# A 30-step recurrent stage: the wide mix, the ten-step Newton chain, and products and transposes in blocks

## The chip, the cores and the metric

The kernel runs on one core of one Trainium2 chip, in one launch. The metric is the device time of that core in microseconds (us), median of a few runs. The core has five engines that each work through their own instructions in order and wait for each other by semaphores: TensorE (PE in the profile, its weight loads are PEld), VectorE (DVE), ScalarE (ACT), GpSimd (POOL) and SyncE (SP), which here only issues DMAs. A DMA is a transfer by one of 16 DMA engines.

## The reference

A graph transformer of two layers on 128 graphs of 128 nodes with 128 channels, all fp32: attention and a mixture of experts in the first layer, attention and a recurrent feed-forward in the second. Only the last part is touched by the change:

```python
def step(h, _):
    h = h + 0.01 * jnp.tanh(h)
    h = h * jax.nn.sigmoid(h)
    h = _layernorm(h, ln_w, ln_b)      # (h - mean) * rsqrt(var + 1e-5) * w + bias, over the channels
    h = jnp.einsum('bsc,dc->bsd', h, W) + b
    return (h, None)
x, _ = jax.lax.scan(step, x, None, length=30)      # then added to the input of this part
```

Each of the 128 x 128 tokens goes through 30 steps, independently of all others.

## The kernel before

The stage is `recurrent_ffn`. The state of all tokens stays in SBUF as `g`, channels on partitions, in 16 chunks of 1024 tokens. A **slot** is one chunk in one of the 30 steps: slot s is step s // 16, chunk c = s % 16, 480 slots in all. An iteration is 16 slots; iterations 0, 1 and the closing one (number 30) are unrolled, 2 to 29 are a loop on every engine. A chunk has two units u = 0, 1 of 512 tokens, one PSUM bank each.

The layernorm is folded: its mean and weight go into the matrix `w_main` beforehand, and only the reciprocal standard deviation of each token (rstd) remains to be applied. What a slot s does:

- **product** (PE, L1253, one fp32 matmul of 128 x 512 per unit, two rows in the trace): `p_y` = `w_main` times the scaled state. `p_y` has room for two slots, so it waits for the mix of slot s - 2 (`bank_taken`), and for POOL's scaling.
- **tanh** (ACT, L1308, per unit): `th` = tanh(`p_y` + bias).
- **mix** (DVE, L1132, per unit, 512 wide): `th` = 0.01 `th` + `p_y`.
- **silu** (ACT, L1312, per unit): writes the new state `g`.
- **transposes** (PE, L1267, four of 128 x 128 per unit): tokens onto partitions, into `p_gt`, which has room for one slot. So the transposes of slot s, unit u, wait for the statistics of slot s - 1, unit u, and for the silu.
- **statistics** (DVE, L1139, two instructions of 256 per unit): the variance parts of 512 tokens.

Four chunks are a **group** of 32 token columns. When its statistics are there, DVE works out rstd by an integer first guess and three Newton steps, a chain of 11 small instructions n = 0 to 10 on 128 x 32 (`newton`, L1147 to L1161), each waiting for the one before. Then PE transposes rstd (L1273, `transpose_rstd`), ACT copies it (L1335), SP stores it to DRAM and reads it back spread over all partitions (`rb`), and POOL multiplies the four chunks of `g` by it (L1074). All that has to be done before the products of the next step, 16 slots later.

The order on each engine is written out by hand. In turn c, working on slot s, before the change: PE does product(s,0), transposes(s-2,0), product(s,1), transposes(s-2,1), and when c % 4 == 1 the transpose of rstd. DVE does mix(s-1,1), statistics(s-2,0), two Newton instructions, mix(s,0), statistics(s-2,1), two Newton instructions. ACT does tanh(s,0), silu(s-1,1), tanh(s,1), silu(s,0). Newton instructions of a group stand in the turns with c % 4 = 2, 3 and 0: four, four and three.

Of the kernel before, what the change touches and what calls it, by code (L numbers as in the profile page):

```python
# [935 lines left out]
def recurrent_ffn(nc, env, x_sb, out_dram, ln_w, ln_b, w_dram, b_dram, N_TILES=128, ITERS=30):  # L936
# [11 lines left out]
    CHAIN, XCHAIN = 11, 12  # L948
    MAGIC = 1597463007.0
    OUTS = 4  # L950

    with ExitStack() as ctx:
# [20 lines left out]
        rstd = sb("rstd", [P, GTILES])  # L973
        rstd_row = sb("rstd_row", [GTILES, 2, P])
# [62 lines left out]
        with nc.Block() as block:  # L1037
# [52 lines left out]
            def _(dve):  # L1090
# [52 lines left out]
                def newton(k, q, n):  # L1143

                    if n == 0:
# [3 lines left out]
                    else:  # L1149
                        dve.wait_ge(s_nw, CHAIN * k + n)  # L1150
                        if n == 1:
                            wait(dve, s_rt, k)
                            ins = nc.vector.tensor_scalar(rstd[:].bitcast(I32), v.bitcast(I32), -0.5, MAGIC,
                                                          ALU.mult, ALU.add)
                        elif n % 3 == 2:
                            ins = nc.vector.tensor_tensor(work, v, rstd[:], ALU.mult)  # L1156
                        elif n % 3 == 0:
                            ins = nc.vector.scalar_tensor_tensor(out=work, in0=work, scalar=-0.5, in1=rstd[:],  # L1158
                                                                 op0=ALU.mult, op1=ALU.mult)
                        else:  # L1160
                            ins = nc.vector.scalar_tensor_tensor(out=rstd[:], in0=work, scalar=1.5, in1=rstd[:],  # L1161
                                                                 op0=ALU.add, op1=ALU.mult)
                    ins.then_inc(s_nw, 1)

                def newton_part(i, c, place):

                    k, q = GROUPS * i + (c - 6) // GC, (c - 6) // GC % GROUPS
                    for n in range(4 * ((c - 6) % GC) + 2 * place, 4 * ((c - 6) % GC) + 2 * place + 2):
                        if n < CHAIN and live_group(k):
                            newton(k, q, n)  # L1170

# [243 lines left out]
```

## Time and profile before

| | us |
|---|---|
| median of 3 runs | 3339.24 (3337.21 to 3339.80) |
| the profiled execution, its own time | 3341.66 |
| its span, first to last instruction | 3339.9 |
| recurrent stage, from about 1800 us to the end | about 1540 |

The busy shares over the whole span (PE 93%, DVE 87%, ACT 71%, POOL 52%) mix the four parts of the model; the change is in the last part alone, so its own stretch is what has to be read. A row of the timeline gives start and duration of an instruction (or of several alike), and in brackets how long its engine sat idle before it and what released it. On DVE and ACT the next instruction starts before the last one's duration is over, so what an instruction costs its engine is the distance of two starts, while who waits for it waits for its end.

### The profile page before, as it was taken

How to read it: one execution, taken by the hardware profiler on the slowest of the kernel's cores; microseconds unless marked ns; L12 is line 12 of the kernel's file. 1: busy time of each engine (PE TensorE's matmuls, PEld its weight loads, DVE VectorE, ACT ScalarE, POOL GpSimd, SP SyncE). 2: the span in 40 equal slices, each digit the busy share in tenths (PEclk: the TensorE clock that was granted, in tenths of full speed). 3: DMA queues.
4: the chain of work that ended last, by engine and by line, in shares of the span. 5: the costliest groups of instructions: out<-in, count | busy, mean ns of one | idle time of the engine just before them, and what ended most of it. 6: DMA issues, size and time to landing. Idle time of an engine off the chain costs nothing. (4 is left out here: it accounts for less than half of the span.)

```text
span 3339.9 us, 67477 instructions
## 1 busy us (share of the span) xinstructions
PE 3091.6 (93%) x16801; PEld 2062.9 (62%) x16801; DVE 2915.5 (87%) x8976; ACT 2377.9 (71%) x4988; POOL 1722.7 (52%) x1101
## 2 busy tenths in 40 slices
PE   7989986999998999999995799999999999999998
PEld 4666665888886777777774544444444444444446
DVE  5777776888887888888887799999999999999997
ACT  4666663444444777777776988888888888888883
POOL 2445444333332111121110388888888877777776
PEclk9999998999999999999996799999999999999999
DMA  4000000000000000000000255454555555454447
GB/s 129 16 16 16 19 13 14 1 0 0 0 0 17 14 13 9 13 13 13 9 6 3 81 182 176 174 174 176 177 177 177 177 177 177 177 177 176 172 173 239
DMA packets 135072, 290.04 MB, mean 87 GB/s; under 512 B 12081, under 2 KB 69601, under 8 KB 135009
## 3 DMA queue, kind: packets, MB, share of 16 engines
q1 hardware_dynamic: 118112, 280.89, 24.5%
q10 hardware_dynamic: 16896, 8.39, 0.9%
q8 instruction: 29, 0.48, 0.1%
q14 instruction: 35, 0.28, 0.0%
HBM read 278.88 MB, written 10.35 MB: 87 GB/s over the span
## 5 line engine op out<-in xcount | busy, mean ns | idle before, releaser
L1074 POOL TENSOR_TENSOR d_g<-d_g,d_rb 128x1024 f32<-128x1024 f32 x480 | 1120.6, 2369 | 380.6 <-DMA d_rb<-d_rstd_rows 380.2
L1253 PE MATMUL d_p_y<-d_g,d_w_main 128*128 128x512 f32 x1856 | 953.2, 595 | 0.1
L1267 PEld LDWEIGHTS d_p_gt<-ident,d_g 128*128 128x128 f32 x3840 | 436.6, 142 | 710.2 <-ACT d_g L1312 657.1
L1312 ACT ACTIVATE d_g<-d_th,d_bias 128x512 f32<-128x512 f32 x928 | 669.7, 722 | 182.1 <-DVE d_th L1132 174.7
L1139 DVE BATCH_NORM_STATS2 d_stats<-d_p_gt 128x6 f32<-128x256 f32 x1920 | 725.1, 419 | 23.1 <-PE d_p_gt L1267 23.0
L1132 DVE SCALAR_TENSOR_TENSOR d_th<-d_th,d_p_y 128x512 f32<-128x512 f32 x960 | 652.3, 680 | 14.2 <-ACT d_th L1308 7.9
L1267 PE MATMUL d_p_gt<-ident,d_g 128*128 128x128 f32 x3840 | 602.3, 280 | 64.9 <-ACT d_g L1312 23.1
L1308 ACT ACTIVATE d_th<-d_p_y,d_bias 128x512 f32<-128x512 f32 x928 | 622.0, 670 | 1.1 <-PE d_p_y L1253 1.0
L514 ACT ACTIVATE a_prob<-a_masked,a_neg_max 128x128 f32<-128x128 f32 x1024 | 327.4, 392 | 111.8 <-DVE a_neg_max L334 111.7
L434 PE MATMUL a_p_s<-a_k_heads,a_q_t 128*128 128x512 f32 x768 | 397.0, 599 | 0.6 <-DVE a_k_heads L310 0.6
L451 PEld LDWEIGHTS a_p_pv<-a_v_ones,a_prob_t 128*128 128x128 f32 x3072 | 375.1, 193 | 10.7 <-issue 10.3
L451 PE MATMUL a_p_pv<-a_v_ones,a_prob_t 128*128 128x17 f32 (+1 forms) x3072 | 376.7, 259 | 3.2 <-DVE a_context L347 2.0
L817 DVE SCALAR_TENSOR_TENSOR x_sb<-m_p_y,m_combine,x_sb 128x128 f32 (+1 forms) x1024 | 311.4, 343 | 68.1 <-PE m_p_y L859 55.2
L906 ACT ACTIVATE m_hidden<-m_p_h,m_cols 128x512 f32<-128x512 f32 x256 | 176.5, 689 | 225.9 <-PE m_p_h L851 225.9
L441 PEld LDWEIGHTS a_p_pt<-ident,a_prob 128*128 128x128 f32 x1536 | 192.4, 141 | 201.6 <-issue 198.5
L1253 PEld LDWEIGHTS d_p_y<-d_g,d_w_main 128*128 128x128 f32 x1856 | 280.4, 191 | 7.2 <-issue 5.7
L859 PEld LDWEIGHTS m_p_y<-m_w_sb,m_hidden 128*128 128x128 f32 x2048 | 266.0, 191 | 25.8 <-issue 3.5
L859 PE MATMUL m_p_y<-m_w_sb,m_hidden 128*128 128x128 f32 x2048 | 270.9, 275 | 0.0
L321 DVE TENSOR_TENSOR a_masked<-a_p_s,a_mask 128x512 f32<-128x512 f32 x256 | 176.1, 688 | 83.7 <-PE a_p_s L434 82.6
L248 POOL TENSOR_TENSOR x_sb<-x_sb,a_out_bias 128x512 f32 (+1 forms) x32 | 42.1, 1316 | 385.7 <-DVE a_masked L321 339.3
L527 ACT COPY a_prob_t<-a_p_pt 128x512 f32<-128x512 f32 x384 | 221.7, 577 | 17.0 <-PE a_p_pt L441 17.0
L230 POOL TENSOR_TENSOR a_rstd<-a_var,minus_half 128x4 f32<-128x4 f32 x64 | 66.3, 1037 | 323.0 <-DVE a_var L292 323.0
(167 smaller groups left out, 4443.7 us busy)
## 6 DMA issues: line engine op xcount, KB each, us to landing
d_rb<-d_rstd_rows SPq DMA_DIRECT2D x480, 512.0 KB, 5.5
a_adj_in<-in_adj_dram SPq DMA_DIRECT2D x64, 256.0 KB, 2.8
out_dram<-d_out_sb ACTq DMA_DIRECT2D x32, 256.0 KB, 3.2
d_rstd_rows<-d_rstd_row SPq DMA_DIRECT2D x120, 16.0 KB, 1.4
m_w_sb<-in_L_ffn_w_dram SPq DMA_DIRECT2D x2, 512.0 KB
x_sb<-in_x_dram SPq DMA_DIRECT2D x1, 256.0 KB, 2.9
a_w_raw<-in_L_gnn_Wq_dram SPq DMA_DIRECT2D x2, 64.0 KB, 2.2
a_w_raw<-in_L_gnn_Wk_dram SPq DMA_DIRECT2D x2, 64.0 KB, 2.1
```

Of the source, the lines that this page charges most:

```text
L434: nc.tensor.matmul(p_s[:, u % 2], q_t[:, par, g * P:(g + 1) * P], k_heads[:, par, g, h0:h0 + HU, :], start=mask_on_vector, stop=True).then ...
L451: last = nc.tensor.matmul(p_pv[:, h, :], prob_t[:, u % 2, h, :], v_ones[:, par, g, h0 + h, :], start=True, stop=True)
L514: last = nc.scalar.activation(prob[:, u % 2, h, :], scores_src[:, u % 2, h, :], ACT.Exp, bias=neg_max[:, u % 2, h:h + 1], scale=EXP_SCALE)
L817: last = nc.vector.scalar_tensor_tensor(out=x_tile, in0=p_y[:, e % 2, t, :], scalar=combine[:, par, t, e:e + 1], in1=x_tile, op0=ALU.mult, ...
L859: last = nc.tensor.matmul(p_y[:, e % 2, t, :], hidden[:, e % 2, t * P:(t + 1) * P], w2_sb[:, e, :], start=True, stop=True)
L1074: nc.gpsimd.tensor_tensor(g[:, c, :], g[:, c, :], rb[:, buf, :], ALU.mult).then_inc(s_gs, 1)
L1132: nc.vector.scalar_tensor_tensor(out=th[:, b, cols(u)], in0=th[:, b, cols(u)], scalar=0.01, in1=p_y[:, b, cols(u)], op0=ALU.mult, op1=ALU. ...
L1139: ins = nc.vector.bn_stats(stats[:, q % 2, (j * CT + t) // 2].rearrange("p a s -> p (a s)"), p_gt[:, t * P:(t + 2) * P].rearrange("p (a c) ...
L1253: nc.tensor.matmul(p_y[:, c % 2, cols(u)], w_main[:], g[:, c, cols(u)], start=True, stop=True).then_inc(s_y, 1)
L1267: ins = nc.tensor.transpose(p_gt[:, t * P:(t + 1) * P], g[:, c, t * P:(t + 1) * P], ident[:])
L1308: nc.scalar.activation(th[:, b, cols(u)], p_y[:, b, cols(u)], ACT.Tanh, bias=col).then_inc(s_th, 1)
L1312: nc.scalar.activation(g[:, c, cols(u)], th[:, c % 2, cols(u)], ACT.Silu, bias=col).then_inc(s_g, 1)
```

## The change

- **Mix 1024 wide.** One instruction for both units. The products of slot s + 2 and both silus of slot s now wait for that one mix, and the mix for the second tanh.
- **A chain of ten.** The first Newton steps are replaced by one step of higher order and a last one of the old kind; a factor of 3/8 is moved into `w_main`. Ten instructions with one PSUM operand on the reading side at most, one at a time in three places of a turn instead of two and two, so that other work stands between any two of them. They take the turns with c % 4 = 2, 3, 0 (three each), and the last, n = 9, stands in the turn with c % 4 = 1, behind statistics(s-2,0).
- **Blocks.** PE: product(s,0), product(s,1), transposes(s-2,0), transposes(s-2,1), transpose of rstd. DVE: statistics(s-2,0), Newton, mix(s), Newton, statistics(s-2,1), Newton. ACT: the copy of rstd, tanh(s,0), tanh(s,1), silu(s-1,0), silu(s-1,1).
- In the closing iteration both halves of a result are added one behind the other.

```diff
-    CHAIN, XCHAIN = 11, 12
+    CHAIN, XCHAIN, PLACES = 10, 12, 3
...
-                def mix(s, b, u):
-                    dve.wait_ge(s_th, units(s, u))
-                    nc.vector.scalar_tensor_tensor(out=th[:, b, cols(u)], in0=th[:, b, cols(u)], scalar=0.01,
-                                                   in1=p_y[:, b, cols(u)], op0=ALU.mult, op1=ALU.add).then_inc(s_u, 1)
+                def mix(s, b):
+                    dve.wait_ge(s_th, units(s, UNITS - 1))
+                    nc.vector.scalar_tensor_tensor(out=th[:, b], in0=th[:, b], scalar=0.01, in1=p_y[:, b],
+                                                   op0=ALU.mult, op1=ALU.add).then_inc(s_u, 1)
...
-                    for n in range(4 * ((c - 6) % GC) + 2 * place, 4 * ((c - 6) % GC) + 2 * place + 2):
-                        if n < CHAIN and live_group(k):
-                            newton(k, q, n)
+                    n = PLACES * ((c - 6) % GC) + place
+                    if n < CHAIN and live_group(k):
+                        newton(k, q, n)
...
                         s = CHUNKS * i + c
-                        if live(s - 1):
-                            mix(s - 1, (c - 1) % 2, 1)
-                        elif last(i):
-                            add_x(c - 1, 1)
                         if live(s - 2):
                             statistics(s - 2, (c - 2) % CHUNKS, 0)
                         newton_part(i, c, 0)
                         if live(s):
-                            mix(s, c % 2, 0)
+                            mix(s, c % 2)
                         else:
                             add_x(c, 0)
+                            add_x(c, 1)
+                        newton_part(i, c, 1)
                         if live(s - 2):
                             statistics(s - 2, (c - 2) % CHUNKS, 1)
-                        newton_part(i, c, 1)
+                        newton_part(i, c, 2)
...
-                        wait(pe, s_u, units(s - 2, u))
+                        wait(pe, s_u, s - 1)
...
-                            if live(s - 2):
+                        if live(s - 2):
+                            for u in range(UNITS):
                                 transpose_g(s - 2, (c - 2) % CHUNKS, u)
...
-                        if live(s):
-                            tanh(s, c % 2, 1, col)
-                            silu(s, c, 0, col)
+                        for u in range(UNITS):
+                            if live(s):
+                                tanh(s, c % 2, u, col)
+                        for u in range(UNITS):
+                            if live(s - 1):
+                                silu(s - 1, (c - 1) % CHUNKS, u, 0.0 if isinstance(i, int) and s - 1 < CHUNKS else bias[:])
```

DVE's row in the loop, in a turn with Newton instructions (c = 3). Names are those of the program: `d_stats` the statistics, `d_p_nw` and `d_rstd` the Newton chain, `d_th` the mix; register instructions set the values that waits compare with. Before:

```order
L1139 BN_STATS d_stats<-d_p_gt 128x6 [waits d_g_transposed]
L1139 BN_STATS d_stats<-d_p_gt 128x6
L1150 REGISTER_ALU
L1161 SCALAR_TENSOR_TENSOR d_rstd<-d_p_nw,d_rstd 128x32 [waits d_newton_chain]
L1150 REGISTER_ALU
L1156 TENSOR_TENSOR d_p_nw<-d_p_nw,d_rstd 128x32 [waits d_newton_chain]
L1131 ISA
L1132 SCALAR_TENSOR_TENSOR d_th<-d_th,d_p_y 128x512 [waits d_tanh_ready]
L1139 BN_STATS d_stats<-d_p_gt 128x6 [waits d_g_transposed]
L1139 BN_STATS d_stats<-d_p_gt 128x6
```

The same turn after (`d_vy` is the new tile `vy2`):

```order
L1142 BN_STATS d_stats<-d_p_gt 128x6 [waits d_g_transposed]
L1142 BN_STATS d_stats<-d_p_gt 128x6
L1155 REGISTER_ALU
L1162 TENSOR_TENSOR d_vy<-d_p_nw,d_rstd 128x32 [waits d_newton_chain]
L1134 ISA
L1135 SCALAR_TENSOR_TENSOR d_th<-d_th,d_p_y 128x1024 [waits d_tanh_ready]
L1155 REGISTER_ALU
L1164 SCALAR_TENSOR_TENSOR d_p_nw<-d_vy,d_p_nw 128x32 [waits d_newton_chain]
L1142 BN_STATS d_stats<-d_p_gt 128x6 [waits d_g_transposed]
L1142 BN_STATS d_stats<-d_p_gt 128x6
```

The pair of linked Newton instructions has become one on each side of a mix that is twice as wide.

PE's row in the loop around the transpose of rstd (`d_p_row`), from the second half of turn c = 1. Before:

```order
L1253 MATMUL d_p_y<-d_g,d_w_main 128x512 [waits d_g_scaled,d_u_ready]
L1267 MATMUL d_p_gt<-ident,d_g 128x128 [waits d_stats_ready,d_g_ready]
L1267 MATMUL d_p_gt<-ident,d_g 128x128 x3
L1271 ISA
L1018 REGISTER_ALU [waits d_newton_chain]
L1273 MATMUL d_p_row<-ident,d_rstd 32x128 [waits d_row_ready]
L1018 ISA
L1252 REGISTER_ALU [waits d_u_ready]
L1253 MATMUL d_p_y<-d_g,d_w_main 128x512 [waits d_g_scaled]
L1267 MATMUL d_p_gt<-ident,d_g 128x128 [waits d_stats_ready,d_g_ready]
L1267 MATMUL d_p_gt<-ident,d_g 128x128 x3
```

After:

```order
L1275 MATMUL d_p_gt<-ident,d_g 128x128 [waits d_stats_ready,d_g_ready]
L1275 MATMUL d_p_gt<-ident,d_g 128x128 x3
L1272 REGISTER_ALU
L1275 MATMUL d_p_gt<-ident,d_g 128x128 [waits d_stats_ready,d_g_ready]
L1275 MATMUL d_p_gt<-ident,d_g 128x128 x3
L1279 ISA
L1021 REGISTER_ALU [waits d_newton_chain]
L1281 MATMUL d_p_row<-ident,d_rstd 32x128 [waits d_row_ready]
L1021 REGISTER_ALU
L1260 REGISTER_ALU [waits d_u_ready]
L1261 MATMUL d_p_y<-d_g,d_w_main 128x512 [waits d_g_scaled]
L1261 MATMUL d_p_y<-d_g,d_w_main 128x512 [waits d_g_scaled,d_u_ready]
```

Behind the transpose of rstd there now stand both products of the next slot, and only then its transposes.

## Rows read from the trace of the kernel before

**Rows 1.** Windows: length, busy (count) of each engine, TensorE's granted clock, DMA.

```profile
1850.00:1900.00 50.00, 32.42 (x153) 26.35 (x154) 32.38 (x99) 45.48 (x104) 16.20 (x7) 0.68 0.24 86
...
2500.00:2600.00 100.00, 95.46 (x412) 48.77 (x411) 97.88 (x292) 87.37 (x144) 83.58 (x37) 1.00 0.49 172
```

**Rows 2.** Groups by line, 1900 to 3300: count | busy, mean ns | idle before.

```profile
L1074 POOL TENSOR_TENSOR d_g<-d_g,d_rb 128x1024 f32<-128x1024 f32 x466 | 1088.1, 2370 | 277.6 <-DMA d_rb<-d_rstd_rows 277.2
...
L1312 ACT ACTIVATE d_g<-d_th,d_bias 128x512 f32<-128x512 f32 x927 | 669.0, 722 | 181.9 <-DVE d_th L1132 174.6
```

**Rows 3.** Timeline of DVE, a turn with two linked Newton instructions.

```profile
2602.15 0.76 DVE L1139 BATCH_NORM_STATS2 d_stats<-d_p_gt 128x6 f32<-128x256 f32 x2
2602.82 0.17 DVE L1161 SCALAR_TENSOR_TENSOR d_rstd<-d_p_nw,d_rstd 128x32 f32<-128x32 f32 x1
2603.03 0.20 DVE L1156 TENSOR_TENSOR d_p_nw<-d_p_nw,d_rstd 128x32 f32<-128x32 f32 x1
2603.15 0.69 DVE L1132 SCALAR_TENSOR_TENSOR d_th<-d_th,d_p_y 128x512 f32<-128x512 f32 x1
2603.75 0.76 DVE L1139 BATCH_NORM_STATS2 d_stats<-d_p_gt 128x6 f32<-128x256 f32 x2
```

**Rows 4.** Timeline of DVE, a Newton instruction that stands alone.

```profile
2620.05 0.18 DVE L1161 SCALAR_TENSOR_TENSOR d_rstd<-d_p_nw,d_rstd 128x32 f32<-128x32 f32 x1
2620.14 0.68 DVE L1132 SCALAR_TENSOR_TENSOR d_th<-d_th,d_p_y 128x512 f32<-128x512 f32 x1
```

**Rows 5.** Timeline of DVE: the same first Newton instruction, one iteration apart.

```profile
2599.61 0.19 DVE L1147 TENSOR_SCALAR d_p_nw<-d_stats 128x32 f32<-128x32 f32 x1
...
2647.72 0.18 DVE L1147 TENSOR_SCALAR d_p_nw<-d_stats 128x32 f32<-128x32 f32 x1
```

**Rows 6.** Timeline of DVE at the loop's branch, between two iterations.

```profile
2616.64 0.19 DVE L1161 SCALAR_TENSOR_TENSOR d_rstd<-d_p_nw,d_rstd 128x32 f32<-128x32 f32 x1
...
2617.16 0.69 DVE L1132 SCALAR_TENSOR_TENSOR d_th<-d_th,d_p_y 128x512 f32<-128x512 f32 x1 [0.32 <-issue]
```

**Rows 7.** Timeline of PE, products and transposes back to back.

```profile
2608.54 1.02 PE L1253 MATMUL d_p_y<-d_g,d_w_main 128*128 128x512 f32 x2
2609.40 0.60 PE L1267 MATMUL d_p_gt<-ident,d_g 128*128 128x128 f32 x4
2609.84 1.02 PE L1253 MATMUL d_p_y<-d_g,d_w_main 128*128 128x512 f32 x2
```

**Rows 8.** Timeline, weight load of transposes that waited; transposes behind it.

```profile
2603.02 0.42 PEld L1267 LDWEIGHTS d_p_gt<-ident,d_g 128*128 128x128 f32 x4 [0.90 <-ACT d_g L1312]
...
2603.05 0.63 PE L1267 MATMUL d_p_gt<-ident,d_g 128*128 128x128 f32 x4
```

**Rows 9.** Timeline, transposes released by statistics, and the product behind them.

```profile
2616.10 0.41 DVE L1139 BATCH_NORM_STATS2 d_stats<-d_p_gt 128x6 f32<-128x256 f32 x1
...
2616.56 0.42 PEld L1267 LDWEIGHTS d_p_gt<-ident,d_g 128*128 128x128 f32 x4 [0.91 <-DVE d_stats L1139]
...
2617.06 0.59 PE L1253 MATMUL d_p_y<-d_g,d_w_main 128*128 128x512 f32 x1
```

**Rows 10.** Closing iteration, DVE and PE: the transpose of rstd waits for Newton.

```profile
3307.07 0.18 DVE L1161 SCALAR_TENSOR_TENSOR d_rstd<-d_p_nw,d_rstd 128x32 f32<-128x32 f32 x1
...
3307.30 0.10 PEld L1273 LDWEIGHTS d_p_row<-ident,d_rstd 128*32 128x32 f32 x1 [3.91 <-DVE d_rstd L1161]
...
3307.49 0.47 PE L1259 MATMUL d_p_y<-d_w_main,d_g 128*128 128x128 f32 x1
```

**Rows 11.** Timeline of PE, transposes and then the product across the loop's branch.

```profile
2613.46 0.63 PE L1267 MATMUL d_p_gt<-ident,d_g 128*128 128x128 f32 x4
2614.06 0.69 PE L1253 MATMUL d_p_y<-d_g,d_w_main 128*128 128x512 f32 x1
```

**Rows 12.** Timeline of ACT in iteration 0.

```profile
1870.92 0.60 ACT L1308 ACTIVATE d_th<-d_p_y 128x512 f32<-128x512 f32 x1 [0.43 <-PE d_p_y L1248]
...
1871.77 0.63 ACT L1312 ACTIVATE d_g<-d_th 128x512 f32<-128x512 f32 x1 [0.26 <-DVE d_th L1132]
```

More of the change, by code:

```diff
@@ L947, in recurrent_ffn @@
     ALL_GROUPS = ITERS * GROUPS
-    CHAIN, XCHAIN = 11, 12
+    CHAIN, XCHAIN, PLACES = 10, 12, 3
     MAGIC = 1597463007.0
+    RSTD_SCALE = 3.0 / 8.0
     OUTS = 4
@@ L973, in recurrent_ffn @@
         rstd = sb("rstd", [P, GTILES])
+        vy2 = sb("vy2", [P, GTILES])
         rstd_row = sb("rstd_row", [GTILES, 2, P])
@@ L1143, in newton @@
                 def newton(k, q, n):
+                    y = rstd[:]
                     if n == 0:
@@ L1152, in newton @@
                             wait(dve, s_rt, k)
[L1153 to L1158, printed above, removed]
+                            ins = nc.vector.tensor_scalar(y.bitcast(I32), v.bitcast(I32), -0.5, MAGIC, ALU.mult, ALU.add)
+                        elif n == 2 or n == 7:
+                            ins = nc.vector.tensor_tensor(work, v, y, ALU.mult)
+                        elif n == 3:
+                            ins = nc.vector.tensor_tensor(vy2[:], work, y, ALU.mult)
+                        elif n == 4:
+                            ins = nc.vector.scalar_tensor_tensor(out=work, in0=vy2[:], scalar=-10.0 / 3.0, in1=work,
+                                                                 op0=ALU.add, op1=ALU.mult)
+                        elif n == 5:
+                            ins = nc.vector.tensor_tensor(work, work, y, ALU.mult)
+                        elif n == 8:
+                            ins = nc.vector.scalar_tensor_tensor(out=work, in0=work, scalar=-0.5 * RSTD_SCALE ** 2, in1=y,
                                                                  op0=ALU.mult, op1=ALU.mult)
                         else:
-                            ins = nc.vector.scalar_tensor_tensor(out=rstd[:], in0=work, scalar=1.5, in1=rstd[:],
+                            ins = nc.vector.scalar_tensor_tensor(out=y, in0=work, scalar=5.0 if n == 6 else 1.5, in1=y,
                                                                  op0=ALU.add, op1=ALU.mult)
@@ L1174, in add_x @@
                     dve.wait_ge(s_y, units(SLOTS + o, u))
+                    dve.wait_ge(s_xb, CHUNKS)
                     wait(dve, s_out[n % OUTS], 16 * (n // OUTS))
@@ L1215, in _ @@
                 link(nc.vector.tensor_scalar(row_sum[:], row_sum[:], 1.0 / P, None, ALU.mult))
-                link(nc.vector.tensor_scalar(w_centred[:], w_centred[:], row_sum[:], float(np.sqrt(P)),
+                link(nc.vector.tensor_scalar(w_centred[:], w_centred[:], row_sum[:], RSTD_SCALE * float(np.sqrt(P)),
                                              ALU.subtract, ALU.mult))
@@ L1226, in _ @@
                 iterations(dve, body)
-                dve.wait_ge(s_xb, CHUNKS)
-                add_x(CHUNKS - 1, 1)
             @block.tensor
@@ L1310, in silu @@
                 def silu(s, c, u, col):
-                    act.wait_ge(s_u, units(s, u))
+                    act.wait_ge(s_u, s + 1)
                     nc.scalar.activation(g[:, c, cols(u)], th[:, c % 2, cols(u)], ACT.Silu, bias=col).then_inc(s_g, 1)
@@ L1324, in body @@
                         s = CHUNKS * i + c
-                        if live(s):
-                            tanh(s, c % 2, 0, col)
-                        if live(s - 1):
-                            silu(s - 1, (c - 1) % CHUNKS, 1, 0.0 if isinstance(i, int) and s - 1 < CHUNKS else bias[:])
                         k, q = GROUPS * i + (c - 10) // GC, (c - 10) // GC % GROUPS
```

1 line of the change is left out of this document (removed).

## The prediction, made before the changed kernel was run

> **What bounds the kernel now.** I read the windows first: they say which part of the kernel a stretch is like. From 1900 us on DVE is busy 97.88 us of 100, PE 95.46, ACT 87.37, at TensorE's full clock, 1.00 or 2.4 GHz [rows 1]. The groups of the same stretch say who waits: ACT's silu sat idle 181.9 us, nearly all of it for the mix on DVE, while POOL's 277.6 us of idle time were waits for its own DMAs [rows 2]. So DVE is asked, and POOL is ahead. The timeline of DVE says what a turn costs it, by distances of starts: a statistics pair 0.67 (2602.15 to 2602.82), the first of two linked Newton instructions 0.21, the second 0.12, a mix 0.60 [rows 3]; a Newton instruction alone 0.09 [rows 4]. There is no gap: 1.60 us per unit with two Newton instructions. A group of four slots is 8 x 0.60 + 8 x 0.67 + 5 pairs x 0.33 + 0.09 = 11.9. An iteration of four groups takes 2647.72 - 2599.61 = 48.11 us [rows 5]; 4 x 11.9 is 47.6, and the loop's branch adds 0.52 - 0.12 = 0.4 [rows 6]. PE has less: a product unit 0.86 and a transposes unit 0.44 [rows 7], 8 x 1.30 + 0.11 for the transpose of rstd = 10.5 per group. DVE is the bound, and PE stands 1.4 behind it.
>
> **The change part by part, on DVE.** Mix: a mix of 512 costs 0.60 and a statistics instruction of 256 half of 0.67, so 256 elements more cost 0.265, and 512 more 0.53: 1.13 per slot in place of 1.20. Its bounds are 1.10 and 1.20 (nothing saved). Newton: ten single instructions with other work between them, at 0.09 to 0.12 each; 0.10 to 0.11 in what follows. The chain's 5 x 0.33 + 0.09 = 1.74 becomes 1.05. A group is then 8 x 0.67 + 4 x 1.13 + 1.05 = 10.9, one us less. The branch, which now follows a single Newton instruction whose wait is met early, should be hidden under the statistics before it: another 0.4 per iteration. If DVE stayed the bound, an iteration would be 43.7 us. That is what must be tested against the waits.
>
> On VectorE I weigh a rule. The starts show that a linked Newton instruction costs 0.21 and an unlinked one 0.09 to 0.12, although each lasts 0.17 to 0.20 [rows 3, 4]. The Trainium skill says otherwise ("VectorE: DVE Perf Modes", on the DRAIN after every op): the next operation does not start before the pipe is empty, and waiting by semaphore costs nothing extra, so only the number of instructions counts. By it every Newton instruction would cost its whole 0.18: DVE's group would be 11.7 instead of 10.9, and the five Newton instructions on the loop below would make it 0.4 longer, which is 29 x 2.0 = 58 us, 3397. The trace does not agree with it at either place, so it gets no chance of its own, and the sum goes by the rows.
>
> **On PE and between the engines.** Group k is slots 4k to 4k + 3. Four rules of the new order matter. Transposes(s,1) wait for statistics(s-1,1), as before, since `p_gt` holds one slot. Behind transposes(s-1,1) on PE there now stand both products of slot s + 2, and only then transposes(s,0). DVE in turn s + 2 starts with statistics(s,0), so it cannot go on without them. And the transpose of rstd stands behind transposes(4k+7,1), waits for n = 9, and has the products of slot 4k + 10 behind it; before, the last Newton instruction was done two units earlier, and nobody waited.
>
> This makes a loop. I add it up, from the start of n = 9 of one group to that of the next.
>
> Leg A, n = 9 to statistics(4k+8,0). The Newton instruction lasts 0.18. From its end to the weight load of the transpose of rstd it is 0.05 in the one place of the trace where PE waited for it (3307.25 to 3307.30 [rows 10]); in the loop the wait stands in a register instruction ahead of it, and the nearest row for a two-stage release is the weight load at 2603.02, 0.11 after the statistics that ended at 2602.91 [rows 3, 8]. I take 0.11. From there to the product 0.19 [rows 10], with two register instructions between them now that the closing iteration does not have: 0.19 to 0.30, taken as 0.23, near the measured end. Two units of product 2 x 0.86 = 1.72, transposes 0.60 [rows 7], to DVE 0.05 (2603.05 + 0.63 to 2603.75 bounds it at 0.07 [rows 8, 3]). Sum 2.89. In that time DVE has 0.09 + 1.13 + 0.67 = 1.9 us of work: it waits 1.0 us.
>
> Leg B, DVE: statistics 0.67, n = 0 0.10, mix 1.13, n = 1 0.11, statistics(4k+8,1) to its end 0.76. Sum 2.77.
>
> Leg C, that end to statistics(4k+10,0): release 0.11 (0.05 where only one semaphore is waited for: 2616.51 to 2616.56), weight load to product 0.50 (2616.56 to 2617.06 [rows 9]), products 1.72, transposes and release 0.65. Sum 2.98. DVE has 2.8 us of work there: it waits 0.15 to 0.2.
>
> Leg D, DVE: 0.67, n = 6 0.10, mix 1.13, n = 7 0.11, 0.67, n = 8 0.10, 0.67, and n = 9 starts. Sum 3.45.
>
> A to D are 12.09 us per group, against 11.9 on DVE before. Four groups are 48.36; PE's own branch lies on leg C once per iteration and costs 0.60 - 0.46 = 0.14 [rows 11]. So 48.50 per iteration against 48.11: **+0.39**, times 29 iterations of this kind = +11.3 us. DVE's saving of 4.4 us per iteration is turned into its waiting.
>
> **Covered or unchanged.** ACT: four units of 0.63 each and the copy, 10.3 per group, each tanh pair ready well before its mix. The wide mix makes silu(s,0) wait for both halves, but silu(s,0) now comes a turn later, with over 1 us to spare. POOL needs rstd 16 slots later, and its idle time stays. Iteration 0 is bound by ACT, whose waits of 0.43 and 0.26 per slot [rows 12] change their places, since the second half's transposes are now not behind the first half's statistics work, but no silu fills the gap; I take 0, with -5 to +5 us for 16 slots. The closing iteration is bound by stores and by the way of the last rstd; 0, with +-2.
>
> **The sum.** The profiled execution took 3341.66 in all, 2.4 above the median of the runs. 3341.7 + 11.3 = 3353.0, and against the median 3339.2 + 11.3 = 3350.5. I predict 3350.
>
> **Rivals.**
>
> *The loop closes faster (not slower).* If the register wait costs no more than the plain one (0.05), the product follows at 0.19, and the release in leg C is 0.05, legs A and C lose 0.16 per group: 11.93, 47.86 per iteration, -7 us. A mix at 1.10 and Newton instructions at 0.09 lose another 0.1 to 0.15: 11.8, 47.3, -23. For it: 0.05 has been seen in both places. Against it: those were waits of one plain semaphore, and the unlike places are exactly those in the loop. Typical: 3332.
>
> *DVE stays the bound (faster).* If statistics(s,0) finds its transposes done, because PE is far enough ahead, the iteration is 43.7 to 44.2: 29 x -4.2 = -120, 3220 us. For it: PE has 10.5 of work per 10.9. Against it: PE cannot be ahead; it is held by statistics(s-1,1) and by n = 9, both of which DVE issues just before.
>
> *Waits cost more (slower by 1%).* Each leg has two hand-overs, and after one the first instructions may start late: at the loop's branch the mix came 0.4 late, although nothing but its issue held it [rows 6], because that could only begin behind the linked Newton instruction. Of such a delay 0.12 in leg A and 0.12 in leg C are 0.25 per group, 49.5 per iteration, +40: 3380. It decides if the product starts later than 0.45 after n = 9 ended. A lower TensorE clock would do the same; in iteration 0, with PE busy 32.42 of 50 us, it was granted 0.68 [rows 1], a mix of 1.2 and 2.4 GHz. Here PE keeps 10.5 of 12.1 us, as before, so that is a small part of it.
>
> *The change does not do on DVE what it says:* the wide mix costs 1.20, no gain. It lies on legs B and D: +0.14 per group, +16 us more, 3366.
>
> **How the numbers follow.** Around 0.2% (6.7 us) is what a measurement of this kernel can tell from no change. Chances: the loop as added up 0.57 (3338 to 3362, of which 0.45 is slower and 0.12 the same); it closes faster 0.22 (0.12 the same, 0.10 faster); DVE stays the bound 0.05; waits cost more 0.11; the wide mix saves nothing 0.05. So faster 0.15, same 0.24, slower 0.61. The range takes in both bounds of the loop, 3326 to 3368; outside are DVE as the bound and most of the costly waits, about 0.15.
>
> **What would show it.** In the timeline of DVE in the loop: a statistics pair with 0.8 to 1.1 us of idle time before it, released by PE's transposes, once per group, behind n = 9, and one of 0.1 to 0.3 two slots later; Newton instructions alone at 0.09 to 0.12; mixes 1.13 before the next start; first Newton instructions 12.1 apart. PE's weight load for rstd waits 0.3 to 0.4 us for n = 9. DVE's busy share falls from 98 to about 90 of 100. Wrong if DVE shows no idle time, if PE's wait for n = 9 is missing, or if an iteration is not 48.1 to 48.9.

## The result, and the profile after

| | before, us | changed, us |
|---|---|---|
| median of 7 runs | 3339.24 | 3351.14 (3348.86 to 3352.08) |
| ratio | | 1.0034, 95% interval 1.0022 to 1.0045 |
| span of the profiled execution | 3339.9 | 3347.1 |
| one iteration of the loop | 48.11 | 48.40 |

The changed kernel is slower by 0.34%; 3350 was predicted. An iteration here and below is the distance of the same first Newton instruction, averaged over 25 iterations of the profiled execution.

The window of [rows 1] and the groups that answer to [rows 2]: length, busy us (count) of PE, PE's weight loads, DVE, ACT, POOL, then clock and DMA; for groups count | busy, mean ns | idle before, and releaser.

```profile
2500.00:2600.00 100.00, 94.21 (x409) 53.20 (x406) 91.10 (x250) 86.16 (x141) 82.76 (x37) 1.00 0.50 176
```

```profile
L1142 DVE BATCH_NORM_STATS2 d_stats<-d_p_gt 128x6 f32<-128x256 f32 x1852 | 698.1, 418 | 126.5 <-PE d_p_gt L1275 115.8
L1317 ACT ACTIVATE d_th<-d_p_y,d_bias 128x512 f32<-128x512 f32 x924 | 633.1, 685 | 196.2 <-PE d_p_y L1261 180.5
L1321 ACT ACTIVATE d_g<-d_th,d_bias 128x512 f32<-128x512 f32 x927 | 613.1, 711 | 0.7 <-DVE d_th L1135 0.7
```

DVE fell from 97.88 to 91.10 us of 100, and no engine rose, PE's weight loads apart (48.77 to 53.20 us): nobody is the bound now. The silu, idle 181.9 us before [rows 2], now 0.7, waits no more; instead the statistics wait for PE's transposes and the tanh for PE's products. The first Newton instructions that answer to [rows 5] (timeline of DVE; an iteration from the first to the last, and the group that holds the loop's branch in the middle):

```profile
2592.24 0.19 DVE L1152 TENSOR_SCALAR d_p_nw<-d_stats 128x32 f32<-128x32 f32 x1
...
2616.26 0.19 DVE L1152 TENSOR_SCALAR d_p_nw<-d_stats 128x32 f32<-128x32 f32 x1
...
2628.62 0.19 DVE L1152 TENSOR_SCALAR d_p_nw<-d_stats 128x32 f32<-128x32 f32 x1
2640.63 0.19 DVE L1152 TENSOR_SCALAR d_p_nw<-d_stats 128x32 f32<-128x32 f32 x1
```

The timeline of DVE and PE (start, duration, engine, line, operation, in brackets the idle time before and its releaser) shows one group:

```profile
2600.72 0.17 DVE L1172 SCALAR_TENSOR_TENSOR d_rstd<-d_p_nw,d_rstd 128x32 f32<-128x32 f32 x1
2600.81 1.21 DVE L1135 SCALAR_TENSOR_TENSOR d_th<-d_th,d_p_y 128x1024 f32<-128x1024 f32 x1
2601.93 0.75 DVE L1142 BATCH_NORM_STATS2 d_stats<-d_p_gt 128x6 f32<-128x256 f32 x2
2603.57 0.76 DVE L1142 BATCH_NORM_STATS2 d_stats<-d_p_gt 128x6 f32<-128x256 f32 x2 [0.89 <-PE d_p_gt L1275]
2604.25 0.18 DVE L1152 TENSOR_SCALAR d_p_nw<-d_stats 128x32 f32<-128x32 f32 x1
2604.35 1.21 DVE L1135 SCALAR_TENSOR_TENSOR d_th<-d_th,d_p_y 128x1024 f32<-128x1024 f32 x1
2605.58 0.75 DVE L1142 BATCH_NORM_STATS2 d_stats<-d_p_gt 128x6 f32<-128x256 f32 x2
...
2609.00 0.18 DVE L1167 TENSOR_TENSOR d_p_nw<-d_p_nw,d_rstd 128x32 f32<-128x32 f32 x1
2609.29 0.76 DVE L1142 BATCH_NORM_STATS2 d_stats<-d_p_gt 128x6 f32<-128x256 f32 x2
```

```profile
2600.94 0.09 PEld L1281 LDWEIGHTS d_p_row<-ident,d_rstd 128*32 128x32 f32 x1 [0.37 <-DVE d_rstd L1172]
```

```profile
2600.94 0.28 PE L1281 MATMUL d_p_row<-ident,d_rstd 128*32 128x128 f32 x1
2601.12 1.98 PE L1261 MATMUL d_p_y<-d_g,d_w_main 128*128 128x512 f32 x4
2602.93 1.04 PE L1275 MATMUL d_p_gt<-ident,d_g 128*128 128x128 f32 x8
...
2606.47 0.63 PE L1275 MATMUL d_p_gt<-ident,d_g 128*128 128x128 f32 x4 [0.34 <-DVE d_stats L1142]
2606.94 1.88 PE L1261 MATMUL d_p_y<-d_g,d_w_main 128*128 128x512 f32 x4
2608.66 1.20 PE L1275 MATMUL d_p_gt<-ident,d_g 128*128 128x128 f32 x8
```

The last Newton instruction (2600.72) releases the transpose of rstd (2600.94), two products and the transposes follow, and only then can DVE start the statistics at 2603.57, after 0.89 idle. From the statistics that end at 2605.58 + 0.75 = 2606.33 the same way is gone again, to 2609.29, where DVE loses another 0.2 (2609.00 to 2609.29 is 0.29, of which the Newton instruction is 0.09).

### The profile page after: what moved, and what is told of

It is laid out like the page before. It is cut to its first block and busy times, and to the rows that moved or that the text cites. A ratio compares the mean times of both kernels' runs of the same rounds, so it can differ in the third digit from the quotient of the medians.

```text
span 3347.1 us, 67133 instructions
## 1 busy us (share of the span) xinstructions
PE 3077.4 (92%) x16801; PEld 2125.3 (63%) x16801; DVE 2822.2 (84%) x8376; ACT 2368.7 (71%) x4988; POOL 1720.5 (51%) x1101
## 5 line engine op out<-in xcount | busy, mean ns | idle before, releaser
L1261 PE MATMUL d_p_y<-d_g,d_w_main 128*128 128x512 f32 x1856 | 887.8, 601 | 0.1
L1317 ACT ACTIVATE d_th<-d_p_y,d_bias 128x512 f32<-128x512 f32 x928 | 635.9, 685 | 199.0 <-PE d_p_y L1261 183.3
L1275 PEld LDWEIGHTS d_p_gt<-ident,d_g 128*128 128x128 f32 x3840 | 453.1, 143 | 375.7 <-issue 326.5
L1275 PE MATMUL d_p_gt<-ident,d_g 128*128 128x128 f32 x3840 | 566.5, 279 | 66.6 <-DVE d_stats L1142 66.6
L1321 ACT ACTIVATE d_g<-d_th,d_bias 128x512 f32<-128x512 f32 x928 | 613.7, 711 | 0.7 <-DVE d_th L1135 0.7
L1135 DVE SCALAR_TENSOR_TENSOR d_th<-d_th,d_p_y 128x1024 f32<-128x1024 f32 x480 | 580.1, 1209 | 3.8 <-ACT d_th L1317 3.8
L1261 PEld LDWEIGHTS d_p_y<-d_g,d_w_main 128*128 128x128 f32 x1856 | 316.3, 190 | 238.5 <-issue 230.2
L441 PE MATMUL a_p_pt<-ident,a_prob 128*128 128x128 f32 x1536 | 230.5, 273 | 0.3 <-ACT a_prob_t L527 0.3
```

Of the source, the lines that this page charges most:

```text
L441: last = nc.tensor.transpose(p_pt[:, h, :], prob[:, b, h, :], ident[:])
L1135: nc.vector.scalar_tensor_tensor(out=th[:, b], in0=th[:, b], scalar=0.01, in1=p_y[:, b], op0=ALU.mult, op1=ALU.add).then_inc(s_u, 1)
L1261: nc.tensor.matmul(p_y[:, c % 2, cols(u)], w_main[:], g[:, c, cols(u)], start=True, stop=True).then_inc(s_y, 1)
L1275: ins = nc.tensor.transpose(p_gt[:, t * P:(t + 1) * P], g[:, c, t * P:(t + 1) * P], ident[:])
L1317: nc.scalar.activation(th[:, b, cols(u)], p_y[:, b, cols(u)], ACT.Tanh, bias=col).then_inc(s_th, 1)
L1321: nc.scalar.activation(g[:, c, cols(u)], th[:, c % 2, cols(u)], ACT.Silu, bias=col).then_inc(s_g, 1)
```

## The experiments

Each was timed beside the kernel before, which then took 3339.7 to 3342.2 us. The changed kernel itself stands at 3351.1 and 48.40.

| | median, us | ratio to before (95%) | iteration, us |
|---|---|---|---|
| e1, transpose of rstd later | 3300.4 | 0.9877 (0.9861 to 0.9894) | 46.45 |
| e2, chain ends one place earlier | 3300.2 | 0.9879 (0.9862 to 0.9895) | 46.51 |
| e9, e1 and e2 | 3298.7 | 0.9872 (0.9856 to 0.9889) | 46.44 |
| e3, last Newton one place later | 3501.2, one run | | 53.37 |
| e7, mix in halves | 3366.9 | 1.0080 (1.0064 to 1.0097) | 48.95 |
| e6, old chain | 3381.9 | 1.0123 (1.0106 to 1.0140) | 49.42 |
| e4, PE alternating | 3355.9 | 1.0047 (1.0031 to 1.0064) | 48.54 |
| e5, before + new chain | 3228.4 | 0.9662 (0.9646 to 0.9678) | 44.28 |
| e8, e5 + blocks on PE | 3250.6 | 0.9728 (0.9712 to 0.9745) | 44.28 |
| e12, e8 without them in iteration 0 | 3231.4 | 0.9670 (0.9654 to 0.9686) | 44.28 |
| e11, mix last in the turn | 3322.9 | 0.9943 (0.9926 to 0.9959) | 47.30 |
| e10, e1 and e11 | 3216.4 | 0.9625 (0.9609 to 0.9641) | 43.69 |

### The wait for the last Newton instruction

**e1.** The transpose of rstd moves behind the next two products (ACT's copy moves behind the tanhs with it).

```diff
+                        k = GROUPS * i + (c - 10) // GC
+                        if c % GC == 2 and live_group(k):
+                            transpose_rstd(k)
                         if live(s - 2):
                             for u in range(UNITS):
                                 transpose_g(s - 2, (c - 2) % CHUNKS, u)
-                        k = GROUPS * i + (c - 9) // GC
-                        if c % GC == 1 and live_group(k):
-                            transpose_rstd(k)
```

> The changed kernel with one thing moved: the transpose of rstd stands one place later on PE, behind both products of the next slot (4k+10) and ahead of its transposes, and ACT copies rstd behind the two tanhs of that turn. Theory (leg A of the sum: the last Newton instruction, the transpose of rstd, two products, transposes, statistics): PE no longer waits for n = 9, the 0.89 us of idle time before statistics(4k+8,0) shrinks to at most 0.5, an iteration takes 46.3 to 46.6 us instead of 48.40, and the whole is 29 x 1.9 = 55 us below the changed kernel, about 3296 us. Rival (it is the width of the mix that holds tanh and silu apart): nothing moves, 3351. Rival (the blocks on PE alone do it, whatever stands between them): leg C takes over fully and less than 20 us come back.

**e2.** The last Newton instruction stands right behind the one before it.

```diff
-                    if n < CHAIN and live_group(k):
+                    if n < CHAIN - 1 and live_group(k):
                         newton(k, q, n)
+                        if n == CHAIN - 2:
+                            newton(k, q, CHAIN - 1)
```

> The changed kernel with PE and ACT untouched: n = 9 follows n = 8 directly at the end of the turn before, as a linked pair, 0.7 us earlier. DVE pays about 0.12 for the link. Theory: PE's weight load for rstd no longer waits 0.37 us; idle time before statistics(4k+8,0) falls from 0.89 to about 0.4, iteration 46.3 to 46.6, about 3296 us, the same as with the transpose of rstd moved. Rival (the place of the transpose on PE costs by itself, not its wait): less than 10 us come back.

**e9.** Both edits.

> The changed kernel with both repairs at once, the transpose of rstd behind the two products and n = 9 linked to n = 8 in the turn before. If both take away one and the same wait, the times do not add up: 46.4 to 46.5 per iteration, 3297 to 3301, as each alone, with leg C (statistics(s,1), two products, transposes) left as the bound. If they were separate costs: another 50 us less, 3250.

**e3.** The opposite: the last Newton instruction one place later, behind the mix.

```diff
+                    if n == CHAIN - 1:
+                        return
+                    if n == CHAIN:
+                        n = CHAIN - 1
```

> The changed kernel with n = 9 one place later, behind the mix of the turn (1.13 + 0.09 us later). If the way of leg A sets the group, all of it shows: 4 x 1.22 = 4.9 us per iteration, 53.3 in place of 48.40, 29 x 4.9 = 142 us more, about 3493 us. If DVE or leg C set the group, most of it is hidden: under 40 us more.

e1 and e2 came to the same time, and e9 to the same again: they take away one and the same wait, about 1.9 us per iteration. e3 costs 4.97 us per iteration. In 20 of 28 iterations it is 4.54: a group takes 13.14 instead of 12.01, and the 1.13 between them are the mix that now stands ahead of n = 9. The other eight iterations are 1.5 us longer still, and they are the eight in which TensorE's granted clock fell for a stretch; the window (columns as in [rows 1]) is of one, at 0.56, near the lower of the two levels. DVE's timeline in e3, with n = 9 in the first row, and the window:

```profile
2601.09 0.19 DVE L1172 SCALAR_TENSOR_TENSOR d_rstd<-d_p_nw,d_rstd 128x32 f32<-128x32 f32 x1
2601.19 0.76 DVE L1142 BATCH_NORM_STATS2 d_stats<-d_p_gt 128x6 f32<-128x256 f32 x2
2604.10 0.76 DVE L1142 BATCH_NORM_STATS2 d_stats<-d_p_gt 128x6 f32<-128x256 f32 x2 [2.16 <-PE d_p_gt L1279]
```

```profile
2335.90:2339.30 3.40, 3.40 (x10) 1.87 (x9) 0.03 (x1) 1.57 (x4) 1.15 (x1) 0.56 0.20 57
```

And in e1, where a smaller wait is left at the same place:

```profile
2599.98 0.76 DVE L1142 BATCH_NORM_STATS2 d_stats<-d_p_gt 128x6 f32<-128x256 f32 x2
...
2602.62 0.76 DVE L1142 BATCH_NORM_STATS2 d_stats<-d_p_gt 128x6 f32<-128x256 f32 x2
2603.81 0.76 DVE L1142 BATCH_NORM_STATS2 d_stats<-d_p_gt 128x6 f32<-128x256 f32 x2 [0.42 <-PE d_p_gt L1275]
```

From the end of statistics(4k+6,1), 2599.98 + 0.76 = 2600.74, to 2603.81 are 3.07 us: leg C's 2.96 and the transpose of rstd, now in it. So a second round, that of leg C, binds once the first is gone: 10.9 + 0.42 + 0.2 = 11.5 per group, where 11.55 was measured.

### The parts of the change on their own

**e7.** The mix in two halves of 512, back to back, each waiting for its own tanh and releasing its own product and silu; everything else as changed. The mix, PE's wait and the silu's wait are edited to match, which is left out here.

```diff
-                            mix(s, c % 2)
+                            mix(s, c % 2, 0)
+                            mix(s, c % 2, 1)
```

> The changed kernel with the mix in two halves of 512, one behind the other in its place, each waiting for its own tanh and releasing its own product and silu; blocks and chain of ten kept. Theory: legs B and D carry 0.07 more each, the waits stay: 48.7 to 48.8 per iteration, 29 x 0.35 = 10 us above the changed kernel, 3361. Rival (the wide mix costs by making silu and products wait for both halves): 10 us or more below the changed kernel.

+0.55 per iteration, 3366.9 us, more than the 0.35 expected. Of four mixes per group two lie on the loop, 2 x 0.07 x 4 = 0.56. The wide mix is a gain, but half of it falls into DVE's waits.

**e6.** The changed order with the chain of eleven and its linked pairs, ahead of the mix and behind statistics(s,1).

```diff
-    CHAIN, XCHAIN, PLACES = 10, 12, 3
+    CHAIN, XCHAIN, PLACES = 11, 12, 3
...
-                    n = PLACES * ((c - 6) % GC) + place
-                    if n < CHAIN and live_group(k):
-                        newton(k, q, n)
+                    for n in range(4 * ((c - 6) % GC) + 2 * place, 4 * ((c - 6) % GC) + 2 * place + 2):
+                        if n < CHAIN and live_group(k):
+                            newton(k, q, n)
```

> The changed kernel with the old chain of eleven in linked pairs (behind statistics(s-2,0) and behind statistics(s-2,1)), blocks and wide mix kept. The last step is then early enough for the transpose of rstd, and PE does not wait for it, but DVE carries 0.7 us more per group. Theory: leg A is gone, leg C stays; 49.0 per iteration, 29 x 0.6 = 17 us above the changed kernel, 3368; DVE waits 0.4 to 0.6 before statistics(4k+8,0). Rival (the new chain is the fault as such): the time of the kernel before or less.

49.42 per iteration, more than expected. DVE still waits, so the linked pairs (2601.53, 2601.74 and 2601.85 are 0.32 together) lie on legs B and D and only in part in a wait:

```profile
2601.53 0.18 DVE L1161 SCALAR_TENSOR_TENSOR d_p_nw<-d_p_nw,d_rstd 128x32 f32<-128x32 f32 x1
2601.74 0.19 DVE L1164 SCALAR_TENSOR_TENSOR d_rstd<-d_p_nw,d_rstd 128x32 f32<-128x32 f32 x1
2601.85 0.75 DVE L1142 BATCH_NORM_STATS2 d_stats<-d_p_gt 128x6 f32<-128x256 f32 x2
...
2607.83 0.76 DVE L1142 BATCH_NORM_STATS2 d_stats<-d_p_gt 128x6 f32<-128x256 f32 x2 [0.53 <-PE d_p_gt L1266]
```

**e4.** PE back in its old order, product and transposes by turns.

```diff
-                        if live(s - 2):
-                            for u in range(UNITS):
+                            if live(s - 2):
                                 transpose_g(s - 2, (c - 2) % CHUNKS, u)
```

> The changed kernel with PE's old order: product(s,0), transposes(s-2,0), product(s,1), transposes(s-2,1); wide mix, chain of ten, DVE and ACT as in the changed kernel. By legs A and C alone each loses a product unit, 0.86, and DVE would be the bound: 43.9 per iteration, 3225 us. But a new way opens, which I think decides: product(s,1) now stands behind transposes(s-2,0), which wait for a silu that ACT issues behind both tanhs of the turn before; from there to the second tanh and the wide mix that waits for it, DVE waits 0.2 before three mixes of a group and 0.7 before the fourth. Expected: about 48.4 per iteration, 3351 us, no better than with the blocks, with DVE's waits before the mix instead of before the statistics. Rival (blocks are the fault by themselves): 3225.

No gain, 5 us slower than expected. The statistics find their transposes done, but the second product is late and with it tanh(s,1), for which the wide mix waits. DVE's timeline:

```profile
2608.03 1.42 DVE L1142 BATCH_NORM_STATS2 d_stats<-d_p_gt 128x6 f32<-128x256 f32 x4
2609.36 0.18 DVE L1152 TENSOR_SCALAR d_p_nw<-d_stats 128x32 f32<-128x32 f32 x1
2610.23 1.22 DVE L1135 SCALAR_TENSOR_TENSOR d_th<-d_th,d_p_y 128x1024 f32<-128x1024 f32 x1 [0.68 <-ACT d_th L1316]
```

**e5.** The kernel before with the chain of ten alone, one instruction behind each mix and each statistics.

```diff
-    CHAIN, XCHAIN = 11, 12
+    CHAIN, XCHAIN, PLACES = 10, 12, 4
...
+                        newton_part(i, c, 0)
                         if live(s - 2):
                             statistics(s - 2, (c - 2) % CHUNKS, 0)
-                        newton_part(i, c, 0)
+                        newton_part(i, c, 1)
                         if live(s):
                             mix(s, c % 2, 0)
                         else:
                             add_x(c, 0)
+                        newton_part(i, c, 2)
                         if live(s - 2):
                             statistics(s - 2, (c - 2) % CHUNKS, 1)
-                        newton_part(i, c, 1)
+                        newton_part(i, c, 3)
```

> The kernel before with the chain of ten alone: its own order on PE and ACT, mixes of 512, and one Newton instruction at each of four places of a turn (behind each mix and behind each statistics pair), so that no two are linked and the last one ends well before the transpose of rstd. Theory: DVE was the bound before and stays it, with no waits, 8 x 0.60 + 8 x 0.67 + 10 x 0.09 = 11.1 us per group, 44.3 per iteration, the branch hidden: 29 x 3.8 = 110 us below the kernel before, about 3229 us. Rival (PE, at 10.5 per group and with waits of its own, takes over at once): 47 or more, under 30 us gained.

**e8.** e5 with PE in blocks.

```diff
-                            if live(s - 2):
+                        if live(s - 2):
+                            for u in range(UNITS):
                                 transpose_g(s - 2, (c - 2) % CHUNKS, u)
```

> The kernel before with the chain of ten at four places, and PE's products and transposes of a slot in blocks (the transpose of rstd behind them as ever); DVE and ACT in the old order, mixes of 512. If blocks cost by themselves, some of the 55 us of leg C should show: 46 per iteration, 3280. If they cost only together with a DVE that begins its turn with statistics(s-2,0), and with n = 9 right ahead of the transpose of rstd, nothing shows: here DVE does a mix and statistics of other units meanwhile, and n = 9 is done two units early. Expected: the latter, 44.3 per iteration, 3229, the same as without the blocks.

**e12.** e8 with the old order in iteration 0.

```diff
+                            if first(i) and live(s - 2):
+                                transpose_g(s - 2, (c - 2) % CHUNKS, u)
-                        if live(s - 2):
+                        if not first(i) and live(s - 2):
```

> e8 (the chain of ten with PE's products and transposes in blocks, 3250.6) with iteration 0 in PE's old alternating order, all others in blocks. Theory: e8 is 22 us behind e5 (3228.4) only because its iteration 0 is longer, and that comes from the order on PE there: then 3229 us, with the first five first-Newton instructions spanning 71 us as in e5. Rival (iteration 0 is longer for another reason, the later iterations' order acting on the closing of the first, or chance of the TensorE clock at that point): 3240 to 3251.

The chain alone takes 3.4% off: DVE has no gap, and an iteration is 44.28, as 8 x (0.60 + 0.67) + 10 x 0.09 = 11.06 per group foretells. The blocks cost nothing in the loop, and 22 us in iteration 0: e12 has them back but for 3. The windows of e5 and then of e8:

```profile
1850.00:1900.00 50.00, 34.43 (x162) 28.04 (x161) 31.66 (x96) 45.73 (x102) 17.52 (x8) 0.66 0.23 85
2500.00:2600.00 100.00, 99.94 (x444) 53.05 (x444) 100.00 (x309) 94.09 (x155) 90.39 (x40) 1.00 0.53 190
```

```profile
1850.00:1900.00 50.00, 26.74 (x114) 21.80 (x114) 23.92 (x78) 36.71 (x85) 9.29 (x4) 0.57 0.12 43
2500.00:2600.00 100.00, 98.70 (x447) 57.96 (x446) 100.00 (x307) 94.12 (x154) 88.89 (x39) 1.00 0.55 190
```

In the first window PE did less, 26.74 against 34.43 us, and so did ACT, 36.71 against 45.73, at a granted clock of 0.57 against 0.66, near the lower of its two levels. Which came first, less work or the lower clock, these runs don't tell.

### Taking both waits away

**e11.** The mix behind both statistics instead of between them.

```diff
                         newton_part(i, c, 0)
+                        if live(s - 2):
+                            statistics(s - 2, (c - 2) % CHUNKS, 1)
+                        newton_part(i, c, 1)
                         if live(s):
                             mix(s, c % 2)
...
-                        newton_part(i, c, 1)
-                        if live(s - 2):
-                            statistics(s - 2, (c - 2) % CHUNKS, 1)
                         newton_part(i, c, 2)
```

> The changed kernel with one edit: in each turn DVE does statistics(s-2,0), statistics(s-2,1) and then the mix, instead of the mix between the two. Theory (two waits of DVE per group, both because PE's statistics-to-statistics round through two products takes about 2.9 us): with the mix last, the round from the end of statistics(s,1) to statistics(s+2,0) is still 2.96, but DVE now has two mixes and two statistics in it, 2 x 1.13 + 2 x 0.67 = 3.6 us, so the small wait is gone; the one behind the last Newton instruction stays, since it still has 2.85 us before it and DVE only 1.9 us of work. A group is 10.9 - 1.9 + 2.85 = 11.9, an iteration 47.4 to 47.6 in place of 48.40: 3351 - 26 = 3325 us. Rival (the order of the mix does not matter, what waits is the wide mix itself for the second tanh, or the order on ACT): 48.4 or more, 3350 us or above, with DVE waiting for ACT ahead of the mix.

**e10.** The same, with the edit of e1.

> The edit of e11 and that of e1 together: mix behind both statistics, and the transpose of rstd one place later, behind the products of the next turn. Theory: each edit takes one of the two waits of a group, and nothing else has a round of over 10.9 us per group, so DVE is busy throughout: 8 x 0.67 + 4 x 1.13 + 10 x 0.105 = 10.9 per group, 43.7 per iteration, under the 44.28 of e5; 3351 - 29 x 4.7 = 3215 us, DVE 100 of 100 us busy. Rival: as e1 and e9, which both ended at 46.45, whatever is done to one of two waits shows up in the other: 46.4, 3300 us. Second rival: PE, busy 10.5 per group without its waits, becomes the bound when it must alternate in blocks: 11.05 or more per group as in e5, 3228 us, with idle time of DVE ahead of the statistics.

e11 is 28 us faster than the changed kernel, e1 51, and both together 135. With the mix last, DVE has two mixes inside leg C's round, 3.6 us of work against 2.96, and the round no longer binds. In e11 the wait behind n = 9 (first row) remains as it was:

```profile
2603.12 0.17 DVE L1172 SCALAR_TENSOR_TENSOR d_rstd<-d_p_nw,d_rstd 128x32 f32<-128x32 f32 x1
2603.21 0.75 DVE L1142 BATCH_NORM_STATS2 d_stats<-d_p_gt 128x6 f32<-128x256 f32 x2
2603.88 1.20 DVE L1135 SCALAR_TENSOR_TENSOR d_th<-d_th,d_p_y 128x1024 f32<-128x1024 f32 x1
2605.97 0.76 DVE L1142 BATCH_NORM_STATS2 d_stats<-d_p_gt 128x6 f32<-128x256 f32 x2 [0.89 <-PE d_p_gt L1275]
```

In e10 it is gone but for 0.13 us; the same four rows, and the window:

```profile
2602.23 0.18 DVE L1172 SCALAR_TENSOR_TENSOR d_rstd<-d_p_nw,d_rstd 128x32 f32<-128x32 f32 x1
2602.32 0.76 DVE L1142 BATCH_NORM_STATS2 d_stats<-d_p_gt 128x6 f32<-128x256 f32 x2
2602.99 1.21 DVE L1135 SCALAR_TENSOR_TENSOR d_th<-d_th,d_p_y 128x1024 f32<-128x1024 f32 x1
2604.25 0.76 DVE L1142 BATCH_NORM_STATS2 d_stats<-d_p_gt 128x6 f32<-128x256 f32 x2
```

```profile
2500.00:2600.00 100.00, 100.00 (x451) 59.51 (x450) 99.75 (x277) 94.98 (x156) 91.24 (x40) 1.00 0.55 198
```

From the mix to the next start are 1.26 us here and 1.13 behind the other mixes. So DVE has 10.8 us of work, by distances of starts, in a group of 10.92: it is the bound, but for that 0.13, at 43.69 per iteration, where the prediction's sum for "DVE stays the bound" was 43.7 to 44.2. PE's busy share of 100.00 does not make it the bound: its rows overlap (a product row lasts 0.59, the next starts 0.43 later), and the prediction's sum for it is 10.5 per group. e10 beats both kernels, by 3.75% the one before and by 4.0% the changed one.

## Why the prediction held

**The mechanism.** The edit frees one us per group on DVE, and a closed loop of DVE and PE takes it back. e5 (the freed time, kept), e1 and e11 (each one wait less) and e10 (both) show it, and e3 shows that what is put ahead of n = 9 is added one for one, 1.13 per group. The signs that the prediction named are there: 0.89 us of idle time behind n = 9 and 0.2 two slots later, PE's weight load waiting 0.37, DVE busy 91.10 of 100.

**The legs, from the rows of the changed kernel.** A, 2600.72 to 2603.57: 2.85, taken 2.89. B, 2603.57 to 2606.33: 2.76, taken 2.77. C, to 2609.29: 2.96, taken 2.98. D, on to the next n = 9 at 2600.72 + 12.01: 3.44, taken 3.45. Together 12.01 against 12.09.

**Inside leg A two errors cancelled.** The release of the transpose of rstd took 0.05 (2600.89 to 2600.94), not 0.11, and the product followed at 0.18, not 0.23; the rival "the loop closes faster" was right in that. In leg C it was not: from the end of the statistics at 2606.33 to the weight load at 2606.44 are 0.11. The 0.11 had been read off a row that doesn't show it: the weight load at 2603.02 [rows 8] names ACT's silu as its releaser, which ended at 2602.98 (2602.26 + 0.72), and not the statistics that ended at 2602.91. But behind this wait the four rows of products took 1.81 (2601.12 to 2602.93) instead of 1.72.

**The branch** was undersized. It adds 0.36 in its group (2616.26 to 2628.62 is 12.36, the next is 12.01), not 0.14: 0.21 in leg C, where PE's branch lies (2616.26 to 2621.51 is 5.25, and 2604.25 to 2609.29 is 5.04), and 0.15 in the leg A behind it (3.00 instead of 2.85). 4 x 12.01 + 0.36 = 48.40, where 48.50 was taken.

**From loop to total: two more errors cancelled.** The spans of the two profiled executions differ by 7.2 us, the medians by 11.9. What sets them apart lies ahead of the change: in the profiled execution of the changed kernel, the fastest of its seven, the stage began 5.2 us earlier, behind parts that are the same in both. The timeline of DVE has the stage's first instruction and the first Newton instruction of iteration 1; before:

```profile
1789.23 6.70 DVE L1101 BATCH_NORM_STATS2 d_stats_x<-x_sb 128x6 f32<-128x256 f32 x20 [1.86 <-PEq L188]
...
1914.44 0.19 DVE L1147 TENSOR_SCALAR d_p_nw<-d_stats 128x32 f32<-128x32 f32 x1
```

After:

```profile
1784.01 6.69 DVE L1104 BATCH_NORM_STATS2 d_stats_x<-x_sb 128x6 f32<-128x256 f32 x20 [1.85 <-PEq L188]
...
1914.94 0.19 DVE L1152 TENSOR_SCALAR d_p_nw<-d_stats 128x32 f32<-128x32 f32 x1
```

From row to row are 125.2 us before and 130.9 after: iteration 0, with the first turns of iteration 1, costs 5.7 more. Then 28 distances of iterations at +0.29 are 8.1, and the tail from the last iteration's first Newton instruction on is 1.3 shorter (77.28 against 78.62). That makes +12.5 for the stage, near the 11.9 of the medians. The prediction had 29 x 0.39 = 11.3 for the loop, 3.2 too much, and 0 for iteration 0, 5.7 too little and outside the -5 to +5 that it allowed. So the mechanism in the loop was right, but that 3350 came within 1.1 us of the median is in part luck.

**What iteration 0 pays for.** The same distance is 129.3 to 132.7 us in all nine experiments on the changed kernel, which keep its order on DVE and ACT but for the place of the mix, of Newton instructions or of the copy of rstd: with PE alternating (e4, 132.0), with halves of the mix (e7, 130.6), with the old chain (e6, 130.0), with the mix last (e11, 130.6). It is 123.7 in e5 and 124.1 in e12, with the old order. So neither PE's order nor the width nor the chain makes the 5.7; the order on DVE and ACT is left, and which of the two it is was not run. TensorE's clock over this distance was 0.67 before and 0.68 after.

**The rivals.** "DVE stays the bound" failed for the reason given, and came true as soon as the two waits were moved (e10). "The wide mix saves nothing" was priced at +16 us; e7 measured +15.8 over the changed kernel. That iteration 0 can cost 22 us from the order on PE alone (e8, 145.7 against 123.7 in e5) was far outside the -5 to +5 that I allowed. With the changed order on DVE and ACT the blocks cost nothing there (130.9 against 132.0 in e4).

**The rule on VectorE.** In the loop of the changed kernel a Newton instruction with other work around it costs 0.09 to 0.10 from start to start, and a linked one 0.21 (2601.53 to 2601.74 in e6). The sentence of the Trainium skill that the prediction weighed ("VectorE: DVE Perf Modes", "The DRAIN you can't avoid") would make both cost the full 0.18. With ten of them, by estimate from these rows, e5's group would be 0.9 longer than the 11.05 that it took. The Trainium skill itself makes an exception on that page, which the prediction left out: an instruction that is not held starts earlier ("Two Vector instructions with no wait between them"). With it, the trace agrees for the instructions that stand alone: they start 0.09 apart from the next though they last 0.17 to 0.20.

**Left open.** The order of DVE and that of ACT were changed together, and the old ACT order with the new one of DVE was not run. e10 keeps ACT's new order but for the copy of rstd and is the fastest, so that order costs nothing in the loop. In iteration 0 it may.

## What to carry to other kernels

Work taken off a bound engine shows in the time only if every round of hand-overs that it stands in has slack: add up each closed round (release, the work on the other engine that stands ahead in its queue, the way back) and set it against the work that the engine has in the meantime. Putting like work in blocks makes each round longer; whether that costs anything depends on the work between its ends, so order the blocks such that the longest instruction falls inside the longest round. Two waits in one loop have to be taken away together: 28 and 51 us singly, 135 both. And before the spans of two executions are compared, see when the changed part began in each: here 5.2 us of their difference lay ahead of it.

## What the runs showed of the hardware

- DVE's records can get longer while the distances of starts stay. The timeline of DVE in e5, where it is busy 100.00 of 100: a Newton instruction lasts 0.30 to 0.39 and a mix of 512 0.80 to 0.88, though the next starts 0.09 and 0.59 later. A full DVE alone does not do it: in e8, also busy 100.00, they last 0.19 to 0.22 and 0.69 to 0.70. Why e5 differs is open. Durations, and busy shares made of them, can't be compared between such kernels, distances of starts can.

```profile
2600.87 0.38 DVE L1166 TENSOR_TENSOR d_p_nw<-d_p_nw,d_rstd 128x32 f32<-128x32 f32 x1
2600.96 0.88 DVE L1134 SCALAR_TENSOR_TENSOR d_th<-d_th,d_p_y 128x512 f32<-128x512 f32 x1
2601.55 0.39 DVE L1171 SCALAR_TENSOR_TENSOR d_rstd<-d_p_nw,d_rstd 128x32 f32<-128x32 f32 x1
```

- The loop's branch on DVE cost 0.4 behind a linked Newton instruction [rows 6]; in e5 and e8, without linked ones, the group with the branch is 11.13 and 11.07, where the others are 11.05 and 11.07.
- The first product behind a wait of PE ran 0.09 longer over two units (1.81 from 2601.12 to 2602.93 in the changed kernel) than one right behind transposes (1.72 from 2606.94 to 2608.66), at the same granted clock of 1.00.
- In e3 PE idled 1.3 to 1.4 us before each transpose of rstd, and the granted clock stayed at 1.00 in most iterations but fell in eight of 28, as between 2335.9 and 2339.3 (0.56), and these eight took 1.5 us longer. Why only these is open. In the changed kernel, where PE waits less, it stayed at 1.00 throughout the loop.
